# Plain float32 matmuls in a long convolution, a filter stage with angles in turns, and loads made in the stage before

## The chip, the cores and the metric

The kernel runs on one core of one Trainium2 chip. The metric is the device time of one execution in microseconds, the median of several runs. In the profile PE is TensorE, PEld its weight loads, DVE VectorE, ACT ScalarE, POOL GpSimd, SP SyncE, whose queue issues all transfers here.

## The reference

The inputs are x (64 x 64 x 1024, batch, head, position), lengths, the parameters of a state-space filter per head, and three weight matrices. What is computed, cut to its core:

```
dtA = A * dt;  Ct = Cc * (exp(dtA) - 1) / A              # per head h and mode n (64 x 64)
K[h, l] = 2 * sum_n real(Ct * exp(dtA * l))              # one filter of 1024 taps per head
y = causal convolution of x with K along l, + x * D,  masked by length
gate, up = quant(y) @ quant(w_gate).T, quant(y) @ quant(w_up).T      # 1024 -> 2752
h = silu(gate) * up
out = x + quant(h) @ quant(w_down).T                     # 2752 -> 1024
```

quant is fake quantisation to 8 bits: a scale from the largest magnitude of a row, rounding, and the scale again.

## The kernel before

There are three stages, each a block in which every engine has its own program and waits on semaphores; between the blocks all engines meet.

**Filters** (`long_filters`). Parameters lie as 32 x 128 tiles (head pairs by modes), on which VectorE does a chain of some 60 small operations: an exponential by polynomial, the angle reduced modulo a full turn in three parts (`reduce_turns`, lines 52 to 62), then Ct through tanh, sines and two complex products (lines 218 to 251). `tick` makes each of them wait for the one before. TensorE transposes four 32 x 128 tiles to columns (line 342). Then, on 128 x 1024 tiles and in two halves of 16 head pairs, VectorE multiplies angles by positions, reduces them again (line 263), ScalarE takes sines (lines 328, 329; a sine table is loaded after the exponential of line 325), and VectorE and GpSimd build tables. exp(dtA l) is split into a coarse and a fine power, so a filter is a product of two 64-row tables: for each of four banks of PSUM (16 heads), TensorE does 2 x 16 matmuls of 32 x 32 (lines 357 to 361), rows 0 to 63 for even heads, rows 64 to 127 for odd ones. ScalarE copies each bank out (line 335) and SP stores it to k_rev in device memory (line 162).

**Convolution and weights** (`convolve_and_pack`), 32 tiles of two heads. For each head (a half tile, `hh`) the filter is loaded as a Toeplitz matrix t of 128 x 1024 whose row p starts one element later (line 510), and x, loaded as 64 rows, is transposed to 128 x 512 (line 861). The convolution (line 875) is, for 8 distances of blocks, a matmul of a 128 x 128 block of t with 512, 448, ... 64 columns of u. To keep accuracy each operand is split in a high part that fits TensorE's reduced float32 type (float32r) and a rest: t_hi (ScalarE, line 657), t_lo (GpSimd, line 611), u_hi (ScalarE, line 663), u_lo (VectorE, line 780), and three matmuls are done per distance. There is one pair of t slots and one x buffer, so the load of the next t waits for t_lo and that of the next x for the transposes. VectorE masks the result (line 788), takes the largest magnitude (line 804), TensorE transposes that (line 899), VectorE makes scales (lines 793 to 800), TensorE spreads the inverse (line 903), VectorE multiplies and rounds to xq (lines 810, 814), SP stores it.

Beside this the weights are quantised and transposed: in tiles 0 to 21 one tile of w_gate and one of w_up each, in tiles 23 to 30 one of w_down (maxima on VectorE, lines 743 to 755; rounding on ScalarE, line 669; back to integers on GpSimd, line 626; transposes on TensorE, line 894; copies on ScalarE, line 683). The order on each engine is written out by hand in its `body(i, par)`. TensorE's is: convolve half 0, transpose of y_max of the tile before, transposes of the next x, transposes of weights, convolve half 1, spread of the inverse, transposes of x, transposes of weights.

**Feed-forward** (`feed_forward`), 32 tiles of 128 rows: bf16 matmuls against weights that lie in on-chip memory whole.

## Time and profile before

| | us |
|---|---|
| median of 3 runs | 1432.2 |
| lowest, highest | 1426.31, 1437.16 |
| profiled execution | 1423.75 |
| its span | 1422.0 |
| TensorE busy in the span | 1298.7 (91%) |
| VectorE busy | 1000.0 (70%) |
| ScalarE busy | 466.8 (33%) |
| GpSimd busy | 490.2 (34%) |

The busy shares are means over three stages with different limits. The page's chain of work that ended last is nearly all in the feed-forward stage, since TensorE works there without a gap, and says little on the first 500 us. Matmuls are pipelined: a record's length has a drain in it that overlaps the next record, so the distance of two starts tells the cost of one in a train, not its length.

### The profile page before, as it was taken

The numbers are of one execution on the slowest core, as the hardware profiler recorded it, in microseconds if no ns is written. First come the engines' busy times: TensorE is split into PE (matmuls) and PEld (weight loads), VectorE is DVE, ScalarE is ACT, GpSimd is POOL, SyncE is SP. The second block draws the span as 40 slices with busy tenths as digits, with TensorE's granted clock in tenths as the row PEclk, the third lists the DMA queues.
The fourth block names the chain that finished last, engine by engine and source line by source line (L and its number), as shares of the span: only waits on it lengthen the run. The fifth ranks groups of instructions, "written<-read, shape, count | busy, mean of one in ns | idle before, by whom it ended". The sixth has DMA issues, their size and how long they took to land.

```text
span 1422.0 us, 21733 instructions
## 1 busy us (share of the span) xinstructions
PE 1298.7 (91%) x7444; PEld 769.8 (54%) x7444; DVE 1000.0 (70%) x1617; ACT 466.8 (33%) x665; POOL 490.2 (34%) x343
## 2 busy tenths in 40 slices
PE   2378888888888799999999999999999999999998
PEld 0377777878878644444444444444444444444443
DVE  7658889798899766556765676567656765676565
ACT  1145555555565322222222222222222222222222
POOL 2257666676677411222122212221222121212220
PEclk9999999999999899999999999999999999999999
DMA  0087776777787422323322332233223322332222
GB/s 4 8 249 232 217 233 199 235 213 215 252 267 236 164 59 65 63 65 70 90 62 65 70 87 65 65 70 87 65 65 70 85 66 65 70 83 68 65 64 74
DMA packets 137599, 161.58 MB, mean 114 GB/s; under 512 B 101644, under 2 KB 101854, under 8 KB 136286
## 3 DMA queue, kind: packets, MB, share of 16 engines
q1 hardware_dynamic: 137566, 161.16, 40.9%
q8 instruction: 18, 0.29, 0.1%
q14 instruction: 15, 0.12, 0.0%
HBM read 113.28 MB, written 25.49 MB: 98 GB/s over the span
## 4 chain that ended last, share of the span: by engine, by line
PE 64%; DVE 0%; ACT 0%; issue 0%
PE ps_o L1113 22%; PE ps_g L1088 21%; PE ps_u L1088 21%; PE ps_t L1098 0%; ACT h_t L1216 0%; DVE ps_o L1168 0%; DVE res L1171 0%
## 5 line engine op out<-in xcount | busy, mean ns | idle before, releaser
L1242 POOL TENSOR_TENSOR h_int<-h,rounder 128x512 bf16<-128x512 f32 x186 | 186.7, 1025 | 698.2 <-ACT h L1207 695.5
L1088 PE MATMUL ps_g<-wgu,rows 128*128 128x512 bf16 (+1 forms) x1536 | 330.8, 359 | 4.5 <-PEq L377 4.5
L1088 PE MATMUL ps_u<-wgu,rows 128*128 128x512 bf16 (+1 forms) x1536 | 329.0, 357 | 0.0
L1113 PE MATMUL ps_o<-wd,h_t 128*128 128x512 bf16 (+1 forms) x1408 | 319.1, 380 | 0.0
L1201 ACT ACTIVATE g_buf<-g_buf 128x512 f32<-128x512 f32 x192 | 112.3, 585 | 596.3 <-DVE g_buf L1139 596.3
L1139 DVE SCALAR_TENSOR_TENSOR g_buf<-ps_g,sx_all,wide 128x512 f32<-128x512 f32 x192 | 132.3, 689 | 242.4 <-PE ps_g L1088 242.4
L1088 PEld LDWEIGHTS ps_g<-wgu,rows 128*128 128x128 bf16 x1536 | 145.0, 98 | 163.6 <-issue 13.2
L1113 PEld LDWEIGHTS ps_o<-wd,h_t 128*128 128x128 bf16 (+1 forms) x1408 | 134.2, 98 | 178.0 <-issue 34.4
L1088 PEld LDWEIGHTS ps_u<-wgu,rows 128*128 128x128 bf16 x1536 | 146.9, 98 | 151.6 <-issue 0.8
L611 POOL TENSOR_TENSOR t_lo<-t_raw,t_hi 128x1024 fp32r<-128x1024 f32 x64 | 162.5, 2540 | 81.2 <-ACT t_hi L657 81.2
L875 PE MATMUL ps_y<-u_hi,t_hi 128*128 128x512 f32 (+7 forms) x512 | 171.8, 336 | 8.1 <-POOL t_lo L611 3.5
L1139 DVE SCALAR_TENSOR_TENSOR u_buf<-ps_u,sx_all,wide 128x512 f32<-128x512 f32 x192 | 132.4, 690 | 63.1 <-PE ps_u L1088 63.1
L875 PE MATMUL ps_y<-u_lo,t_hi 128*128 128x512 f32 (+7 forms) x512 | 170.2, 332 | 0.0
L875 PE MATMUL ps_y<-u_hi,t_lo 128*128 128x512 f32 (+7 forms) x512 | 168.6, 329 | 0.0
L1207 ACT ACTIVATE h<-h,h_inv 128x512 f32<-128x512 f32 x192 | 118.4, 664 | 80.5 <-DVE h_inv L1160 80.5
L626 POOL TENSOR_TENSOR w_int<-wide,rounder 128x1024 bf16<-128x1024 f32 (+1 forms) x68 | 124.5, 1836 | 54.1 <-ACT wide L669 45.1
L1149 DVE TENSOR_TENSOR h<-g_buf,u_buf 128x512 f32<-128x512 f32 x192 | 138.8, 723 | 0.0
L1151 DVE TENSOR_REDUCE h_max<-h 128x1 f32<-128x512 f32 x192 | 121.1, 631 | 6.6
L875 PEld LDWEIGHTS ps_y<-u_hi,t_hi 128*128 128x128 f32 x512 | 104.6, 204 | 15.0 <-issue 8.2
L875 PEld LDWEIGHTS ps_y<-u_lo,t_hi 128*128 128x128 f32 x512 | 104.1, 203 | 4.9
L875 PEld LDWEIGHTS ps_y<-u_hi,t_lo 128*128 128x128 f32 x512 | 103.5, 202 | 4.9
L657 ACT ACTIVATE t_hi<-t_raw 128x1024 fp32r<-128x1024 f32 x64 | 67.6, 1056 | 116.7 <-DMA t_raw<-k_rev 116.3
(149 smaller groups left out, 1024.5 us busy)
## 6 DMA issues: line engine op xcount, KB each, us to landing
t_raw<-k_rev SPq DMA_DIRECT2D x64, 512.0 KB, 5.9
rows<-in_x SPq DMA_DIRECT2D x64, 256.0 KB, 3.9
res<-in_x SPq DMA_DIRECT2D x64, 256.0 KB, 3.9
out_x<-res SPq DMA_DIRECT2D x64, 256.0 KB, 3.2
wide<-in_L_ffn_w_gate SPq DMA_DIRECT2D x22, 512.0 KB, 6.2
wide<-in_L_ffn_w_up SPq DMA_DIRECT2D x22, 512.0 KB, 7.4
wide<-in_L_ffn_w_down SPq DMA_DIRECT2D x8, 1376.0 KB, 7.6
xq_dram<-xq SPq DMA_DIRECT2D x32, 256.0 KB, 5.8
```

What stands on the lines that cost most here:

```text
L611: pool.tensor_tensor(t_lo[:, hh, :], t_raw[:, hh, :], t_hi[:, hh, :].bitcast(F32), ALU.subtract).then_inc(t_lo_done, 1)
L626: pool.tensor_tensor(out, src, rounder[:].to_broadcast([P, out.shape[1]]), ALU.subtract).then_inc(w_int_ready, 1)
L657: act.activation(t_hi[:, hh, :], t_raw[:, hh, :], ACT.Copy).then_inc(t_hi_done, 1)
L875: last = pe.matmul(out[:, dist * B:NC * B], t[:, hh, block_cols], u[:, hh, 0:n], start=(dist == 0 and k == 0), stop=(dist == NC - 1 and k ...
L1088: last = pe.matmul(bank[:, 0:n], xq[:, par, c, :], wgu[:, NC - 1 - c, first + cols.start:first + cols.stop], start=(c == 0), stop=(c == NC ...
L1113: last = pe.matmul(ps_o[o][:], h_t[0:width, c, :], wd[0:width, c, o * W:(o + 1) * W], start=(c == 0), stop=(c == FC - 1))
L1139: dve.scalar_tensor_tensor(out=buf[:, j % 2, 0:n], in0=bank[:, 0:n], scalar=sx, in1=s[:, cols], op0=ALU.mult, op1=ALU.mult).then_inc(gu_sc ...
L1149: dve.tensor_tensor(h[:, par, cols], g_buf[:, j % 2, 0:n], u_buf[:, j % 2, 0:n], ALU.mult).then_inc(h_ready, 1)
L1151: dve.tensor_reduce(h_max[:, par, j:j + 1], h[:, par, cols], X, ALU.max, apply_absolute_value=True).then_inc(h_maxed, 1)
L1201: act.activation(g_buf[:, j % 2, 0:n], g_buf[:, j % 2, 0:n], ACT.Silu).then_inc(silu_done, 1)
L1207: act.activation(h[:, par, cols], h[:, par, cols], ACT.Copy, scale=h_inv[:, par:par + 1], bias=ROUND).then_inc(h_rounded, 1)
L1242: pool.tensor_tensor(h_int[:, piece(j)], h[:, par, piece(j)], rounder[:].to_broadcast([P, n]), ALU.subtract).then_inc(h_int_ready, 1)
```

## The change

In the filter stage: the angle is kept as a fraction of a turn, so that the large tiles are reduced with one rounding and one subtraction in place of six operations, and the factor 2 pi is the scale of ScalarE's sine; a part of the small products goes to GpSimd, started before ScalarE's results are there; the last matmuls alternate between the two halves of the rows instead of finishing one bank after the other; working tiles move to the memory of wgu, so that the buffers of the next stage are free. SP loads x and weights of tiles 0 and 1 in this stage, and, once the first two banks are stored, their t.

In the convolution stage: one plain float32 matmul per distance on t as loaded and u as copied, in place of three; t has four slots and x two buffers. t_hi, t_lo, u_lo and their semaphores go.

```diff
-def reduce_turns(dve, tick, phase, turns, bound):
+def reduce_turns(dve, tick, phase, angle, turns, bound):
 ...
+def load_toeplitz(sp, k_rev, toep, t_loaded, i, par, hh, L, KROW):
+    slot = 2 * par + hh
+    src = bass.AP(tensor=k_rev.tensor, offset=(2 * i + hh) * KROW, ap=[[1, P], [1, L]])
+    sp.dma_start(toep[:, slot, :], src).then_inc(t_loaded[slot], 16)
+def load_rows(sp, x, x_bufs, x_loaded, i, par, B):
+    for hh in range(2):
+        sp.dma_start(x_bufs[par][hh * B:(hh + 1) * B, :],
+                     x[:, bass.ds(2 * i + hh, 1), :].squeeze(1)).then_inc(x_loaded[par], 16)
 ...  long_filters, SP
+            for i in range(2):
+                load_rows(sp, x, x_bufs, x_loaded, i, i, B)
+            for i in range(2):
+                for g, w in enumerate((w_gate, w_up)):
+                    sp.dma_start(w_f32[:, unit_slot(d, i, g)], w[i * P:(i + 1) * P, :]).then_inc(w_loaded[2 * i + g], 16)
             sp.wait_ge(consts_ready, 1)
 ...
             for b in range(len(ps_k)):
+                if b == 2:
+                    sp.wait_ge(k_stored, 48)
+                    for i in range(2):
+                        for hh in range(2):
+                            load_toeplitz(sp, k_rev, toep, t_loaded, i, i, hh, L, d["KROW"])
 ...  VectorE, small tiles
-            tick(dve.tensor_scalar(s(HALF), s(BB), 0.5, None, ALU.mult))
-            reduce_turns(dve, tick, s(HALF), s(TURN), 3.1415925)
+            reduce_turns(dve, tick, s(RED), s(BB), s(TURN), 3.1415925)
+            tick(dve.tensor_scalar(s(FRAC), s(RED), 1.0 / (2 * math.pi), None, ALU.mult))
 ...
+            dve.wait_ge(pool_small, 3)
+            tick(dve.reciprocal(s(NORM), s(NORM)))
+            for part in (W_RE, W_IM):
+                tick(dve.scalar_tensor_tensor(out=s(part), in0=s(part), scalar=2.0, in1=s(NORM), op0=ALU.mult, op1=ALU.mult))
             dve.wait_ge(act_small, 3)
 ...
-            (lines 231 to 251: norm, its reciprocal, two complex products, scalings)
+            tick(dve.scalar_tensor_tensor(out=s(T0), in0=s(IM), scalar=-1.0, in1=s(W_IM), op0=ALU.mult, op1=ALU.mult))
+            tick(dve.tensor_tensor(s(CT_RE), s(RE), s(W_RE), ALU.mult))
+            tick(dve.tensor_tensor(s(CT_RE), s(CT_RE), s(T0), ALU.add))
+            tick(dve.tensor_tensor(s(T0), s(RE), s(W_IM), ALU.mult))
+            tick(dve.tensor_tensor(s(CT_IM), s(IM), s(W_RE), ALU.mult))
+            tick(dve.tensor_tensor(s(CT_IM), s(CT_IM), s(T0), ALU.add))
 ...  large tiles
-            for kind in range(2):
-                tick(dve.tensor_tensor(phase[:, kind], over(1), powers[:, kind], ALU.mult))
             for half, hs in enumerate(halves):
-                reduce_turns(dve, tick, phase[:, :, hs], turns[:, :, hs], 3.1415925)
+                for kind in range(2):
+                    tick(dve.tensor_tensor(phase[:, kind, hs], over(1)[:, hs], powers[:, kind, hs], ALU.mult))
+                tick(dve.tensor_scalar(turns[:, :, hs], phase[:, :, hs], ROUND, ROUND, ALU.add, ALU.subtract))
+                tick(dve.tensor_tensor(phase[:, :, hs], phase[:, :, hs], turns[:, :, hs], ALU.subtract))
 ...  GpSimd
+            for out, left, right in ((NORM, s(A_RE), s(A_RE)), (N_IM, a_im[:], a_im[:]),
+                                     (W_RE, c_re, s(A_RE)), (C0, c_im, a_im[:]),
+                                     (W_IM, c_im, s(A_RE)), (C1, c_re, a_im[:])):
+                pool.tensor_tensor(s(out), left, right, ALU.mult).then_inc(pool_products, 1)
+            pool.wait_ge(pool_products, 6)
+            (three sums and differences of these)
 ...  TensorE
+            for half in range(2):
+                for j in range(HB):
+                    for hp in range(2):
+                        rows = slice(N * hp, N * hp + N)
+                        pe.matmul(ps_k[2 * half + hp][:, j, :], high_re[rows, first + j, :], cosine[rows, 1, first + j, :],
+                                  start=False, stop=False, skip_group_check=True)
+                    for hp in range(2):
+                        ...  the same with high_im and sine, stop=True
 ...  convolve_and_pack, SP
-                    sp.wait_ge(x_turned, 2 * i + 4)
-                    load_x(i + 2)
-                    sp.wait_ge(t_lo_done, 2 * i + 3)
-                    load_t(i + 2, 0)
+                    sp.wait_ge(x_turned, 2 * i + 2)
+                    load_x(i + 2, par)
+                    sp.wait_ge(conv_done, 2 * i + 1)
+                    load_t(i + 2, par, 0)
 ...
-                    sp.wait_ge(t_lo_done, 2 * i + 4)
-                    load_t(i + 2, 1)
+                    sp.wait_ge(conv_done, 2 * i + 2)
+                    load_t(i + 2, par, 1)
 ...  TensorE
-                    parts = ((t_hi, u_hi), (t_hi, u_lo), (t_lo, u_hi))
-                    for k, (t, u) in enumerate(parts):
-                        last = pe.matmul(out[:, dist * B:NC * B], t[:, hh, block_cols], u[:, hh, 0:n],
-                                         start=(dist == 0 and k == 0), stop=(dist == NC - 1 and k == 2),
-                                         skip_group_check=True)
+                    last = pe.matmul(out[:, dist * B:NC * B], toep[:, slot, block_cols], u[:, hh, 0:n],
+                                     start=(dist == 0), stop=(dist == NC - 1), skip_group_check=True)
```

## Rows read from the trace of the kernel before

**Rows 1.** Busy times by stretch: engines, clock, DMA share, GB/s.
```profile
70.46:97.54 27.08, 17.85 (x120) 16.53 (x120) 12.64 (x19) 12.09 (x14) 14.91 (x7) 1.00 0.80 241
97.54:368.47 270.93, 235.12 (x1744) 214.34 (x1744) 230.68 (x353) 144.91 (x167) 184.89 (x84) 0.92 0.72 223
368.47:484.37 115.90, 103.03 (x781) 92.79 (x782) 103.58 (x140) 67.79 (x78) 85.12 (x42) 0.94 0.71 227
...
499.07:1422.00 922.93, 916.10 (x4502) 426.46 (x4502) 592.16 (x998) 229.07 (x392) 186.79 (x187) 1.00 0.30 70
```

**Rows 2.** TensorE's waits, 97.54 to 368.47 us: total, times, longest.
```profile
PE ps_m L899 <- DVE y_max L804: 22.3, 13, 2.3
PE ps_m L899 <- DMA rows<-in_x: 8.9, 7, 2.1
```

**Rows 3.** Timeline of TensorE, one half tile: start, length, what.
```profile
122.15 0.30 PE L899 MATMUL ps_m<-ident,y_max 128*128 128x128 f32 x1 [0.64 <-DVE u_lo L780]
...
123.45 0.47 PE L875 MATMUL ps_y<-u_hi,t_hi 128*128 128x512 f32 x1
...
126.99 0.28 PE L875 MATMUL ps_y<-u_hi,t_lo 128*128 128x64 f32 x1
127.10 0.36 PE L903 MATMUL ps_i<-diag,ones 128*128 128x128 f32 x1
```

**Rows 4.** VectorE's groups, 97.54 to 368.47 us: busy, mean ns, idle before.
```profile
L804 DVE TENSOR_REDUCE y_max<-y 128x128 f32<-128x1024 f32 x21 | 41.3, 1965 | 0.0
L814 DVE TENSOR_SCALAR xq<-y 128x1024 bf16<-128x1024 f32 x21 | 31.4, 1496 | 2.3
L788 DVE TENSOR_TENSOR y<-ps_y,mask 128x512 f32<-128x512 f32 x42 | 28.9, 687 | 5.1 <-PE ps_y L875 4.1
L780 DVE TENSOR_TENSOR u_lo<-ps_x,u_hi 128x512 fp32r<-128x512 f32 x42 | 28.7, 684 | 27.9 <-ACT u_hi L663 27.9
L810 DVE TENSOR_TENSOR y<-y,ps_i 128x1024 f32<-128x1024 f32 x21 | 25.4, 1211 | 0.0
```

**Rows 5.** Timeline of TensorE, the plain float32 matmuls of line 347.
```profile
25.49 7.03 PE L347 MATMUL ps_k<-d_rows,last_one 1*32 1x512 f32 x8
```

**Rows 6.** Timeline of TensorE, the plain float32 matmul of line 903.
```profile
258.80 0.47 PE L903 MATMUL ps_i<-diag,ones 128*128 128x128 f32 x2
259.20 0.71 PE L861 MATMUL ps_x<-ident,rows 64*128 64x64 f32 x8
```

**Rows 7.** Timeline of the filter stage's small operations.
```profile
14.13 0.21 DVE L218 TENSOR_SCALAR small<-small 32x128 f32<-32x128 f32 x1 [0.63 <-ACT small L322]
...
18.05 0.28 DVE L231 TENSOR_TENSOR small<-small 32x128 f32<-32x128 f32 x1
...
18.99 0.94 DVE L234 RECIPROCAL small<-small 32x128 f32<-32x128 f32 x1
...
24.96 0.60 PE L342 MATMUL ps_cols<-ident,small 32*128 32x32 f32 x4 [24.96 <-DVE small L251]
```

**Rows 8.** Timeline of the filter stage's large tiles.
```profile
33.79 1.28 ACT L328 ACT_TABLE_LOAD   x1
...
38.61 1.04 ACT L329 ACTIVATE cosine<-wide 128x1024 f32<-128x1024 f32 x1
...
43.61 1.23 DVE L270 SCALAR_TENSOR_TENSOR cosine<-cosine 128x1024 f32<-128x1024 f32 x1
```

**Rows 9.** Timeline of the end of the filter stage and the next start.
```profile
59.03 1.64 DVE L281 TENSOR_TENSOR wide<-wide 128x512 f32<-128x512 f32 x1
...
67.66 0.59 ACT L335 ACTIVATE wide<-ps_k 32x512 f32<-32x512 f32 x1 [2.64 <-PE ps_k L360]
...
70.46 0.35 SPq L510 DMA_DIRECT2D t_raw<-k_rev  x1
...
77.70 1.60 PE L861 MATMUL ps_x<-ident,rows 64*128 64x64 f32 x16 [10.14 <-DMA rows<-in_x]
80.32 0.77 PE L875 MATMUL ps_y<-u_hi,t_hi 128*128 128x512 f32 x1 [1.02 <-DVE u_lo L780]
```

More of the change, by code:

```diff
@@ L49, in split_dims, with unit_slot @@
     )
[L52 removed]
+def unit_slot(d, par, u):
+    start = par * (2 * d["F"] - 2 * d["L"]) + u * d["L"]
+    return slice(start, start + d["L"])
+def reduce_turns(dve, tick, phase, angle, turns, bound):
     c1 = 6.28125
@@ L57, in reduce_turns @@
     c3 = 2 * math.pi - c1 - c2
-    tick(dve.tensor_scalar(turns, phase, 1.0 / (2 * math.pi), ROUND, ALU.mult, ALU.add))
+    tick(dve.tensor_scalar(turns, angle, 1.0 / (2 * math.pi), ROUND, ALU.mult, ALU.add))
     tick(dve.tensor_scalar(turns, turns, ROUND, None, ALU.subtract))
-    for part in (c1, c2, c3):
-        tick(dve.scalar_tensor_tensor(out=phase, in0=turns, scalar=-part, in1=phase, op0=ALU.mult, op1=ALU.add))
+    for source, part in ((angle, c1), (phase, c2), (phase, c3)):
+        tick(dve.scalar_tensor_tensor(out=phase, in0=turns, scalar=-part, in1=source, op0=ALU.mult, op1=ALU.add))
     tick(dve.tensor_scalar(phase, phase, bound, -bound, ALU.min, ALU.max))
+def load_toeplitz(sp, k_rev, toep, t_loaded, i, par, hh, L, KROW):
[6 more added lines that the diff above has]
+                     x[:, bass.ds(2 * i + hh, 1), :].squeeze(1)).then_inc(x_loaded[par], 16)
 def long_filters(nc, d, log_dt, C, log_A_real, A_imag, D, lengths, k_rev, ident, ones, identb, rounder, mask, scratch,
-                 rows):
+                 x, w_gate, w_up, w_f32, toep, x_bufs, t_loaded, x_loaded, w_loaded):
     H, B, L, NC = d["H"], d["B"], d["L"], d["C"]
@@ L95, in long_filters @@
         size = 2 * H2 * R
-        phase, turns = (scratch[:, k * size:(k + 1) * size].rearrange("p (k h r) -> p k h r", k=2, h=H2)
-                        for k in range(2))
-        decay = sb("decay", [P, 2, H2, R])
-        sine = sb("sine", [P, 2, H2, R])
-        cosine = sb("cosine", [P, 2, H2, R])
-        high_re = scratch[:, 2 * size:2 * size + H2 * R].rearrange("p (h r) -> p h r", h=H2)
-        high_im = rows[:].rearrange("p (h r) -> p h r", h=H2)
+        phase, turns, decay, sine, cosine, high = (
+            scratch[:, k * size:(k + 1) * size].rearrange("p (k h r) -> p k h r", k=2, h=H2) for k in range(6))
+        high_re, high_im = high[:, 0], high[:, 1]
         d_row = sb("d_row", [1, H])
@@ L140, in over, with s @@
             return cols[:, k, :].unsqueeze(2).to_broadcast([P, H2, R])
+        (A_RE, A, FRAC, RED, TURN, TANH, EM1, EXPA, RE, IM, SIN, COS, NORM, T0, CT_RE, CT_IM,
+         W_RE, W_IM, N_IM, C0, C1, BB) = range(22)
+        def s(k):
+            return small[:, k, :]
         count = [0]
@@ L317, in _ @@
         def _(act):
-            act.wait_ge(dve_step, reached["half"])
-            act.activation(small[:, 10, :], small[:, 3, :], ACT.Sin).then_inc(act_small, 1)
-            act.activation(small[:, 11, :], small[:, 3, :], ACT.Sin, scale=0.5).then_inc(act_small, 1)
-            act.activation(small[:, 5, :], small[:, 1, :], ACT.Tanh, scale=0.5).then_inc(act_small, 1)
+            act.wait_ge(dve_step, reached["reduced"])
+            act.activation(s(SIN), s(RED), ACT.Sin, scale=0.5).then_inc(act_small, 1)
+            act.activation(s(COS), s(RED), ACT.Sin, scale=0.25).then_inc(act_small, 1)
+            act.activation(s(TANH), s(A), ACT.Tanh, scale=0.5).then_inc(act_small, 1)
             flat = "p k h r -> p (k h r)"
@@ L340, in _ @@
             pe.wait_ge(dve_step, reached["small"])
-            for k, src in enumerate((1, 2, 14, 15)):
-                last = pe.transpose(ps_cols[:, k, :], small[:, src, :], ident[0:H2, 0:H2])
+            for k, src in enumerate((A, FRAC, CT_RE, CT_IM)):
+                last = pe.transpose(ps_cols[:, k, :], s(src), ident[0:H2, 0:H2])
             last.then_inc(cols_done, 1)
@@ L392, in convolve_and_pack @@
         s_rows = sb("s_rows", [GU_UNITS + DOWN_TILES, P])
-        t_raw = sb("t_raw", [P, 2, L])
-        t_hi = sb("t_hi", [P, 2, L], F32R)
-        t_lo = sb("t_lo", [P, 2, L], F32R)
-        u_hi = sb("u_hi", [P, 2, NC * B], F32R)
-        u_lo = sb("u_lo", [P, 2, NC * B], F32R)
+        u = sb("u", [P, 2, NC * B])
         y = sb("y", [P, 2, NC, 2, B])
@@ L652, in _, with take_u @@
         def _(act):
-            def t_high(i, hh):
-                act.wait_ge(t_loaded[hh], 16 * i + 16)
-                if not isinstance(i, int) or i >= 1:
-                    act.wait_ge(conv_done, 2 * i + hh - 1)
-                act.activation(t_hi[:, hh, :], t_raw[:, hh, :], ACT.Copy).then_inc(t_hi_done, 1)
-            def u_high(i, hh):
+            def take_u(i, hh):
                 act.wait_ge(x_turned, 2 * i + hh + 1)
@@ L814, in quantise_y @@
                 dve.tensor_scalar(xq[:], v, ROUND, ROUND, ALU.add, ALU.subtract).then_inc(xq_ready, 1)
-            for hh in range(2):
-                u_low(0, hh)
             first_max(0, 0)
```

163 lines of the change are left out of this document (58 added, 105 removed).

## The prediction, made before the change was run

> **What bounds the kernel now.** I read the busy times by stage first [rows 1]. The stretch from 499.07 us on, 923 us, is the feed-forward stage: TensorE is busy for 916 us of it at full clock, and nothing in the change touches it. All that can move lies in the 499 us before: the filter stage up to 70.46, the start of the convolution stage up to 97.54, and then that stage proper, whose cuts at 97.54, 368.47 and 484.37 are the starts of the 1st, 22nd and 31st transpose of y_max (line 899, one per tile). So 21 tiles that also prepare gate and up weights take 270.93 us, 12.90 us each, and the next nine take 115.90, 12.88 each.
>
> Then I asked what a period is made of. TensorE is idle for 270.93 - 235.12 = 35.8 us [rows 1], 1.70 per tile, nearly all of it before the y_max transpose, for y_max itself or for the x rows [rows 2]. The granted clock is 0.92, so 8% of 12.90, 1.03 us per tile, is lost to the lower level (1.2 GHz). Work at full clock is the rest, 12.90 - 1.70 - 1.03 = 10.17 us. A half tile at full clock confirms it: y_max transpose at 122.15, first convolution matmul at 123.45, next step at 127.10, so 1.3 us of transposes and 3.65 us of convolution [rows 3]. In the nine later tiles the same sum is 12.88 - 1.43 (idle) - 0.77 (clock 0.94) = 10.68 us.
>
> VectorE is the other long engine. In those 21 tiles it waits 27.9 us for u_hi and 4.1 for convolutions [rows 4], 1.5 per tile, so its serial work is 11.4 us. TensorE and VectorE wait for each other in turns; neither is saturated.
>
> **The convolution arithmetic.** Removed per half tile: ScalarE's copy to t_hi, GpSimd's subtraction t_lo, VectorE's u_lo (0.68 us [rows 4]), and 24 reduced float32 matmuls. Added: 8 plain float32 matmuls. A plain one appears as two records: the 4 matmuls of 512 columns at line 347 are 8 records in 7.03 us [rows 5], 0.85 us each with the last one's drain. That is 1024 columns at 1.2 GHz (an estimate; the clock column reads 1.00 there, but TensorE had done nothing until then and the spacing tells more), two passes per record. At full clock a record of n columns should take 2n / 2.4 GHz, 0.43 us for 512. A weight load of 128 columns sets a floor: the records at 126.99 and 127.10 start 0.11 us apart, with only 64 columns between them [rows 3]. With 15 ns of overhead per record, a half tile is 2 x (0.115 + 0.122 + 0.175 + 0.228 + 0.282 + 0.335 + 0.388 + 0.442) = 4.17 us for n = 64 to 512, against 3.65: **+0.52 us per half**. The lower bound is the pure stream of 2304 columns in four passes, 3.84 us. The upper bound is the plain pair at line 903: 0.40 us from its start to the next instruction, where 128 columns need 0.21 [rows 6]; if all 8 matmuls kept that 0.19 us, a half would take 5.35. I take 4.17: the pair stands alone before a change of row group, while a train of matmuls can load under the stream, as the reduced one does.
>
> **Waits and buffers.** x gets a second buffer, so its load is released a tile earlier, ahead of the waits for convolutions on SP's queue, and the x part of [rows 2] goes. t gets four slots that are matmul operands as loaded; a slot's load waits for conv_done and has nearly two tiles, over 20 us, until its use. Behind that wait on SP stand the second weight load and the xq store, both wanted a tile later. DMA was 0.72 busy at 223 GB/s [rows 1]; the same bytes in 11.2 us make 0.83, about what the start already shows (0.80). What of y_max? After a second half's convolution VectorE does mask 0.69, quantise 1.2 and 1.5, reduction 2.0 [rows 4], 5.4 us. TensorE has 0.4 + 1.1 + 4.17 = 5.7 us of its own before it asks for y_max, so that wait should all but vanish. VectorE's work falls to 11.4 - 2 x 0.73 = 9.9 us, and with t_lo gone GpSimd is less in its way. Without waits I expect the full clock, as in the long dense stage.
>
> Period with gate and up weights: 10.17 + 1.04 = 11.2, gain 21 x 1.7 = **35.7 us**. The nine others: 9 x (10.68 + 1.04) = 105.5, plus 3.6 us for the waits for scale rows, which I leave in: 109.1 against 115.9, gain **6.8 us**. The last half: +0.5.
>
> **The filter stage.** VectorE's small operations are serial, 0.31 us each. Those from 18.05 to 24.96 (6.9 us [rows 7]) make way for six (1.9) and, earlier, for a reciprocal (0.97) and two more (0.63), of which 0.63 us falls into the idle time before 14.13. Nine operations go to GpSimd, which idles there. The added scaling replaces a removed one. Gain 6.9 - 1.9 - 1.6 + 0.6 = 4.0. From 24.96 on VectorE needed 18.65 us, until 43.61, for both halves' phases [rows 8]. The new first phase is two multiplies of 512 columns, a rounding and a subtraction: 3.3 us by the widths of [rows 4], twice that if GpSimd is in the way. So ScalarE binds: its table load ends 10.1 us after 24.96, two sines of 1.05 add 2.1, and VectorE goes on 12.2 us after instead of 18.65: gain 6.4. The 17.1 us of tables stay. They end at 60.67 - 10.4 = 50.3.
>
> Alternating row halves: the last two banks' 64 matmuls (128 records) took about 6.9 us in order, 54 ns per record, before the last copy at 67.66 [rows 9]. Alternated, both banks end together, and two copies of 0.59 follow: +0.6 if nothing overlaps, -2.8 if two row halves run side by side. No row shows the alternation; the nearest are these, so I take +0.6.
> By the Trainium skill, "TensorEngine Tiling (Array Packing)", rules on tiles, different tiles can load weights and multiply in parallel; by it the stage would end 3.4 us sooner than in my sum, and no row here shows it.
>
> **The start.** The next block begins at 50.3 + 9.8 + 0.6 = 60.7 in place of 70.46, if the early loads don't delay the last k_rev stores. SP issues eight loads of x and weights at its beginning, 0.35 us or a little more each [rows 9], long before the first bank is copied; the four t loads, 2.1 MB, come between the stores, 8.7 us at 241 GB/s [rows 1], about the time until the last stores: nothing, or up to 3 us. With x, t and weights in place the convolution waits only for transposes of x and one copy: 80.32 - 77.70 less u_lo, 1.9 us, instead of 9.86. The first half runs at the low level as now: 7.7 us by [rows 5]. Then 1.3, 4.2, 1.3, 4.2, and y_max 0.4, together 21.0. The first y_max transpose comes at 81.7 instead of 97.54: gain **15.8 us**.
>
> Sum: -35.7 - 6.8 - 15.8 + 0.5 = **-58 us**. The profiled execution took 1423.75 (span 1422.0), 8.5 below the median of 1432.2. It would become 1366, the median 1374.
>
> **Rivals.**
> VectorE stays the pace (0.20): if GpSimd holds the xq operation up so that y_max comes 6.6 us after the convolution, TensorE waits 0.9 in each tile, the period is 12.1, the gain 30 x 0.8 + 16 = 40: 1392. For it: y_max is the largest wait today. Against it: 1.3 us of slack per tile, and more than half of GpSimd's work gone.
> The plain matmul's fixed cost is not hidden (0.07): halves of 5.35, period 13.6, 30 x 0.7 - 16 + 3 = +8: 1440, no difference. For it: [rows 6]. Against: [rows 9], where short plain records follow each other without a gap.
> The clock (0.06), the case of a slower kernel: if each tile's first half, which follows 1.3 us of light transposes, ran at 1.2 GHz it would take 7.7 us and the period 14.7: 30 x 1.8 - 16 = +38, 1470. It decides from a mean half of 5.4 us, a third of each at the low level. Against it: what precedes the low level today is a wait, and the waits go.
> The early loads push the k_rev stores out, or half of the filter gain fails (0.07): 1374 + 8 = 1382.
>
> **Numbers.** Forecast 1374 at 0.60, its own range 1356 (halves of 3.84 us, row halves side by side) to 1388 (halves of 4.4). The 8-in-10 range is 1353 to 1404: it takes in VectorE's case and the late stores, and leaves out the two cases of a long convolution. A measurement of this kernel can tell about 1%, 14 us, from nothing: faster by more 0.87, within 0.07, slower 0.06.
>
> **What would show it.** Right: convolution halves of 4.2 us, a granted clock above 0.97 and TensorE idle for under 0.3 us per tile in the stage proper, first convolution matmul near 62.6 us, periods of 11.2 and 11.7. Wrong: halves over 5 us, a clock of 0.9, or waits of a microsecond for y_max.

## The result: 1352.0 us, and the profile after

The changed kernel takes 1352.04 us (median of 4 runs, 1351.77 to 1353.31) where the kernel before took 1432.92 in the same comparison (1426.31 to 1437.16): ratio 0.9441, 95% interval 0.9404 to 0.9478. The gain is 81 us. I had forecast 1374 and a range from 1353, so the result lies 1 us below the range. The direction and the main mechanisms were right; the sizes were not, nearly all to the same side.

The profiled execution took 1353.31 with a span of 1351.2, against 1423.75 and 1422.0 before. Busy times by stretch come first; the cuts are again the starts of the y_max transposes of tiles 1, 22 and 31 (columns as in [rows 1]).

```profile
57.90:78.82 20.92, 18.75 (x97) 12.84 (x97) 9.96 (x14) 8.47 (x10) 7.53 (x4) 0.78 0.50 157
78.82:305.06 226.24, 226.24 (x1409) 162.87 (x1409) 176.60 (x310) 107.17 (x124) 75.72 (x40) 1.00 0.92 267
305.06:412.97 107.91, 102.85 (x639) 73.08 (x639) 88.27 (x122) 51.94 (x60) 44.17 (x24) 1.00 0.78 227
```

The 21 tiles with gate and up weights take 226.24 us, 10.77 each where [rows 1] gave 12.90. TensorE is busy for all of it at clock 1.00: the waits of [rows 2] and the lost clock are both gone. The nine later tiles take 11.99 each in place of 12.88. The first y_max transpose starts at 78.82 in place of 97.54. The feed-forward stage is as before. Three stretches make up nearly the whole change of the span, in us:

| | forecast | measured |
|---|---|---|
| 21 tiles | -35.7 | -44.7 |
| nine tiles | -6.8 | -8.0 |
| until the first y_max transpose | -15.8 | -18.7 |
| last half, end | +0.5 | +0.6 |
| span | -58 | -70.8 |

One tile on TensorE, from y_max transpose to y_max transpose (start, length, what), answers to [rows 3]:

```profile
78.82 0.28 PE L873 MATMUL ps_m<-ident,y_max 128*128 128x128 f32 x1
...
80.13 4.16 PE L850 MATMUL ps_y<-u,toep 128*128 128x512 f32 x16
84.13 0.44 PE L877 MATMUL ps_i<-diag,ones 128*128 128x128 f32 x2
...
85.60 4.16 PE L850 MATMUL ps_y<-u,toep 128*128 128x512 f32 x16
89.59 0.28 PE L873 MATMUL ps_m<-ident,y_max 128*128 128x128 f32 x1
```

The convolution half goes from 80.13 to 84.13, 4.00 us from start to start (4.16 includes the last one's drain). Its weight loads show why it isn't 4.17:

```profile
204.59 0.19 PEld L850 LDWEIGHTS ps_y<-u,toep 128*128 128x128 f32 x1 [0.24 <-issue]
205.02 0.19 PEld L850 LDWEIGHTS ps_y<-u,toep 128*128 128x128 f32 x1 [0.24 <-issue]
205.39 0.19 PEld L850 LDWEIGHTS ps_y<-u,toep 128*128 128x128 f32 x1 [0.19 <-issue]
```

Between the loads for 512 and for 448 columns lie 0.43 us, then 0.37: 2 x 512 and 2 x 448 columns at 2.4 GHz take 0.427 and 0.373. Nothing is left for an overhead per record; what the half takes above the pure stream of 3.84 us comes from the records of 64 columns, which follow each other at 0.11 to 0.12 us as the weight loads do in [rows 3]. VectorE's groups in the same 226 us answer to [rows 4]:

```profile
L788 DVE TENSOR_REDUCE y_max<-y 128x128 f32<-128x1024 f32 x21 | 40.6, 1933 | 0.0
L772 DVE TENSOR_TENSOR y<-ps_y,mask 128x512 f32<-128x512 f32 x42 | 28.9, 687 | 43.4 <-PE ps_y L850 43.4
...
L798 DVE TENSOR_SCALAR xq<-y 128x1024 bf16<-128x1024 f32 x21 | 14.6, 694 | 2.3
L784 DVE TENSOR_SCALAR diag<-ident,t_inv 128x128 f32<-128x128 f32 x21 | 6.0, 286 | 0.7
```

u_lo is gone, and the same xq operation takes 694 ns in place of 1496. VectorE now waits 43.4 us for convolutions, 2.07 per tile, so its serial work is 10.77 - 2.07 = 8.7 us a tile; TensorE alone sets the pace. Last, the filter stage and the start (timeline of VectorE, TensorE and ScalarE):

```profile
23.05 0.29 DVE L276 COPY cols<-ps_cols 128x128 f32<-128x128 f32 x1 [0.86 <-PE ps_cols L373]
...
33.54 1.23 DVE L290 SCALAR_TENSOR_TENSOR wgu<-wgu 128x1024 f32<-128x1024 f32 x1
...
50.65 0.32 PE L391 MATMUL ps_k<-wgu 64*32 64x32 f32 x4 [4.92 <-DVE wgu L301]
...
54.14 1.06 ACT L366 ACTIVATE wgu<-ps_k 32x512 f32<-32x512 f32 x2 [7.26 <-PE ps_k L395]
...
59.78 1.57 PE L837 MATMUL ps_x<-ident,rows 64*128 64x64 f32 x16 [5.73 <-PEq L94]
61.64 6.96 PE L850 MATMUL ps_y<-u,toep 128*128 128x512 f32 x16 [0.29 <-ACT u L655]
68.53 0.71 PE L837 MATMUL ps_x<-ident,x_more 64*128 64x64 f32 x8
```

The last 64 matmuls run from 50.65 to the copy at 54.14, 3.5 us, where the order before took 6.9 [rows 9]. The block starts at 59.78, the first convolution at 61.64.

### The profile page after: what moved, and what is told of

Same layout as the page of the kernel before. It is cut to its first block, busy times and chain, and to the rows that moved or that the text cites. A ratio compares the mean times of both kernels' runs of the same rounds, so it can differ in the third digit from the quotient of the medians.

```text
span 1351.2 us, 20322 instructions
## 1 busy us (share of the span) xinstructions
PE 1284.5 (95%) x6932; PEld 687.5 (51%) x6932; DVE 918.9 (68%) x1536; ACT 409.4 (30%) x601; POOL 335.5 (25%) x288
## 4 chain that ended last, share of the span: by engine, by line
PE 68%; DVE 0%; ACT 0%; issue 0%
PE ps_o L1087 23%; PE ps_g L1062 22%; PE ps_u L1062 22%; PE ps_t L1072 0%; ACT h_t L1190 0%; DVE ps_o L1142 0%; DVE res L1145 0%
## 5 line engine op out<-in xcount | busy, mean ns | idle before, releaser
L850 PE MATMUL ps_y<-u,toep 128*128 128x512 f32 (+7 forms) x1024 | 269.4, 417 | 2.3 <-ACT s_rows L719 1.0
L1062 PEld LDWEIGHTS ps_g<-wgu,rows 128*128 128x128 bf16 x1536 | 145.0, 98 | 163.6 <-issue 13.2
L850 PEld LDWEIGHTS ps_y<-u,toep 128*128 128x128 f32 x1024 | 177.5, 192 | 89.5 <-issue 58.1
L630 POOL TENSOR_TENSOR w_int<-wide,rounder 128x1024 bf16<-128x1024 f32 (+1 forms) x68 | 127.4, 1884 | 222.2 <-ACT wide L661 160.2
L772 DVE TENSOR_TENSOR y<-ps_y,mask 128x512 f32<-128x512 f32 x64 | 44.1, 689 | 70.8 <-PE ps_y L850 68.4
L655 ACT ACTIVATE u<-ps_x 128x512 f32<-128x512 f32 x64 | 38.1, 597 | 136.3 <-PE ps_x L837 136.3
L661 ACT ACTIVATE wide<-wide,w_inv 128x1024 f32<-128x1024 f32 x44 | 50.2, 1144 | 39.9 <-DVE w_inv L758 39.9
L788 DVE TENSOR_REDUCE y_max<-y 128x128 f32<-128x1024 f32 x32 | 61.6, 1926 | 0.1
L1142 DVE SCALAR_TENSOR_TENSOR ps_o<-ps_o,h_s,s_down 128x512 f32<-128x512 f32 x64 | 48.0, 750 | 9.9 <-DMA res<-in_x 8.3
L1145 DVE TENSOR_TENSOR res<-ps_o,res 128x512 f32<-128x512 f32 x64 | 44.2, 691 | 2.2
```

Of the source, the lines that this page charges most:

```text
L630: pool.tensor_tensor(out, src, rounder[:].to_broadcast([P, out.shape[1]]), ALU.subtract).then_inc(w_int_ready, 1)
L661: act.activation(w_f32[:, cols], w_f32[:, cols], ACT.Copy, scale=w_inv[:, par, u:u + 1], bias=ROUND).then_inc(w_rounded, 1)
L788: dve.tensor_reduce(y_max[:], y[:, par].rearrange("p c h b -> p (h b) c"), X, ALU.max, apply_absolute_value=True).then_inc(y_max_done, 1)
L850: last = pe.matmul(out[:, dist * B:NC * B], toep[:, slot, block_cols], u[:, hh, 0:n], start=(dist == 0), stop=(dist == NC - 1), skip_group ...
L1062: last = pe.matmul(bank[:, 0:n], xq[:, par, c, :], wgu[:, NC - 1 - c, first + cols.start:first + cols.stop], start=(c == 0), stop=(c == NC ...
```

## The experiments

Medians are in us. The kernel before, measured again beside each group of runs, had 1431.9 to 1432.3 with the first twelve kernels and 1435.9 with the last three (e13 to e15); the ratio is against it. Theory A is each time the account that I held, drawn from the prediction and the trace after.

**1. The parts alone.** First the new filter stage without early loads, on the old convolution:

```diff
 (before) + long_filters and reduce_turns of the change, no early loads of x, weights, t
```

> The kernel before with the new filter stage alone (angles in turns, products on GpSimd, alternating row halves), without the loads in it, and the old convolution stage. Theory A (the filter stage's gain passes through whole and has nothing to do with the convolution): the convolution stage's first load is issued at 57 us instead of 70.46, the period per tile stays at 12.9 us, the time is 13 us lower, 1420. Rival (the start of the convolution stage swallows it): 1432. If the 81 us of the whole change came mostly from here, it would be 1352.

Measured 1422.4 (1412.8 to 1431.9), ratio 0.9891 (0.983 to 0.9952). The first y_max transpose came at 85.63, 11.9 sooner, but the 21 tiles then took 13.65 each in place of 12.90 at a clock of 0.88 in the profiled execution, which was the slowest of the four. The old loop, in which two engines wait for each other and the clock falls, is unsteady (the four executions lie 19 us apart), and in the profiled one it gave back more than the start had gained; the median kept 9.5 us.

Then the buffers alone, with all arithmetic as before: four t slots, but still one x buffer, each half of which is reloaded as soon as it has been transposed.

```diff
-        t_raw = sb("t_raw", [P, 2, L]);  t_lo = sb("t_lo", [P, 2, L], F32R)
+        t_raw = sb("t_raw", [P, 4, L], F32R)          # t_lo is written over it
-                    sp.wait_ge(t_lo_done, 2 * i + 3)
+                    sp.wait_ge(conv_done, 2 * i + 1)   # and x reloaded half by half
```

> The kernel before with its three reduced float32 matmuls and all the splitting kept, but with four t slots (t_lo written over the raw slot) and each half of x reloaded as soon as that half has been transposed; filter stage as before. Theory A (the wait for each other of TensorE and VectorE was a matter of late loads as well as of VectorE's work): the x waits go, and VectorE's own serial work of 11.4 us per tile becomes the period: 11.5 instead of 12.9, 42 us less, 1390. Rival B (buffers are all): period 10.2, TensorE's own work, 1350. Rival C (the splitting work on VectorE and GpSimd is all): period 12.5, 1420.

Measured 1407.1, ratio 0.982 (0.9766 to 0.9874): between A and C. Its windows, VectorE's groups and TensorE's waits over 21 tiles:

```profile
100.00:361.72 261.72, 232.16 (x1745) 212.65 (x1745) 247.20 (x351) 145.89 (x167) 183.21 (x83) 0.92 0.77 232
```
```profile
L815 DVE TENSOR_SCALAR xq<-y 128x1024 bf16<-128x1024 f32 x21 | 36.5, 1740 | 2.3
L801 DVE TENSOR_SCALAR diag<-ident,t_inv 128x128 f32<-128x128 f32 x21 | 30.6, 1457 | 0.7
```
```profile
PE ps_m L900 <- DVE y_max L805: 28.5, 19, 2.3
```

The waits for x rows are gone, and VectorE takes their place: it waits for convolutions for 6.2 us in all, so its work is (261.72 - 6.2) / 21 = 12.2 us a tile, where it was 11.4 in the kernel before. The two operations above account for it: they took 1496 [rows 4] and 770 ns before,

```profile
L800 DVE TENSOR_SCALAR diag<-ident,t_inv 128x128 f32<-128x128 f32 x21 | 16.2, 770 | 0.7
```

1740 and 1457 here, and 694 and 286 after the change. Buffers alone were worth 25 us; the rest needs the arithmetic. Between the profiled executions it is 17.8 us, and 11.2 of them lie in the nine later tiles, which took 11.64 us each in this run, less than the 11.99 after the whole change.

**2. The matmul itself.** Three reduced matmuls per distance as before, but on unsplit operands, so that only TensorE's part of the old arithmetic is there (values less accurate):

```diff
+                    for k in range(3):
+                        last = pe.matmul(... start=(dist == 0 and k == 0), stop=(dist == NC - 1 and k == 2))
```

> The changed kernel with three reduced float32 matmuls per distance on the unsplit operands in place of the one plain float32 matmul (the values are less accurate; nobody splits). It has the matmuls of before and the waits, buffers and helpers of after. Theory A (in the changed kernel TensorE alone sets the period of 10.77 us, and a plain half costs 4.00 us against 3.65): period 10.07, 31 x 0.7 = 22 us less, 1330. Rival (DMA, 0.92 busy at 267 GB/s between the cuts, is the bound just behind): period stays above 10.5, 1345 or more.

Measured 1331.2, ratio 0.9277 (0.9232 to 0.9322), period 10.05, with the DMA engines 0.96 busy at 286 GB/s: the rival in which they bound the loop just behind TensorE is out. The plain matmul is thus the dearer one by 0.73 us a tile, 0.36 per half: 4.00 against the 3.65 of [rows 3]. The gain of the change comes from what surrounds the matmuls, in spite of them.

**3. The other engines' work put back**: VectorE's operation of 512 columns per half, GpSimd's of 1024, or both.

```diff
+    dve.tensor_tensor(u_extra[:, hh], ps_x[hh][:], mask[:], ALU.mult)               # VectorE's
+    pool.tensor_tensor(t_extra[:], t_extra[:], t_extra[:], ALU.subtract)            # GpSimd's
```

> The changed kernel with one more VectorE operation of 512 columns per half tile at the place of u_lo (0.69 us, it reads the transposed x in PSUM, and TensorE waits for it before the next transposes, as before). Theory A: VectorE waits 2.07 us per tile in the changed kernel, 1.45 more work fits in it in the 21 gate tiles, the period stays 10.77; in the nine others, where it already makes TensorE wait 0.6 us, up to 1.4 each: 1352 + 0 to 12, 1358. Rival C (VectorE's work passes through whole): 31 x 1.4 = 43 us more, 1395.

> The changed kernel with only GpSimd's extra operation per half tile. Theory A (what GpSimd's work costs is VectorE's time, 2.2 us per tile at most): VectorE 8.7 + 2.2 = 10.9 us per gate tile against TensorE's 10.77: period 10.8 to 11.1, 1352 + 2 to 10, 1358. Rival (GpSimd's work doesn't touch VectorE): 1352.

> The changed kernel with both helpers' work put back as idle work: VectorE's operation of 512 columns per half tile at u_lo's place, and a GpSimd operation of two 1024-column float32 operands per half tile at t_lo's place; convolution, buffers and early loads as changed. Theory A (VectorE becomes the bound as in the kernel with buffers only, where the xq and diag operations took 1.74 and 1.46 us beside GpSimd instead of 0.69 and 0.29): 8.7 + 1.45 + 2.2 = 12.4 us per gate tile, 34 us more in all, 1390. Rival (the work fits into VectorE's 2.07 us of waiting, as alone): 1360.

Measured: VectorE's 1358.6 (0.9467), GpSimd's 1371.2 (0.9571), both 1365.5 (0.9535). I had expected 1358 of GpSimd's, and both to cost most. VectorE's met its number (1358) but not its reason: I had put all of the cost in the nine later tiles, and it lies in the 21, whose period is 11.04 (5 us), with 1 us in the nine. In the 21 tiles of the run with GpSimd's operation alone:

```profile
L813 DVE TENSOR_SCALAR xq<-y 128x1024 bf16<-128x1024 f32 x21 | 46.2, 2198 | 2.3
```
```profile
PE ps_m L888 <- DVE y_max L803: 15.3, 20, 0.9
...
DVE y L787 <- PE ps_y L865: 30.7, 22, 3.8
```

and with both:

```profile
L820 DVE TENSOR_SCALAR xq<-y 128x1024 bf16<-128x1024 f32 x21 | 33.0, 1570 | 2.3
```
```profile
PE ps_m L903 <- DVE y_max L810: 9.8, 19, 0.6
...
DVE y L794 <- PE ps_y L880: 2.5, 3, 1.4
```

VectorE has 30.7 us to spare with GpSimd's alone, and yet TensorE waits for it in 20 of 21 tiles. It isn't VectorE's sum of work that costs there but one chain: the quantising operation, held up by GpSimd, stands right ahead of the maximum that TensorE's next transpose needs. With both put back it is the sum: VectorE waits only 2.5 us, its work is 11.29 us a tile, and the period is 11.41. That xq is held up less there (1570 ns), so that both cost less than GpSimd's alone, I put down to VectorE coming to it at another moment; no run isolates that. If the chain is what costs with GpSimd's alone, it must go when the maximum is taken first:

```diff
-                if last_one:
-                    max_y(i, par)
+                max_y(i, par)
                 ...  quantise_y(i - 1, 1 - par)
-                if not last_one:
-                    max_y(i, par)
```

> The kernel with GpSimd's subtraction put back (1371.2: 19 us more than the kernel after the change, 15.3 of them as TensorE's waits for y_max), and VectorE taking the maximum before it quantises. Theory A: GpSimd's work costs time only through the quantising operation, which it slows from 0.7 to 2.2 us and which stands ahead of the maximum that TensorE waits for; with the maximum first that chain is cut: at most 1358, period at most 11.0 in the 21 tiles, waits for y_max gone. Theory B: GpSimd's work slows something else that TensorE needs (the mask multiplies, its own scaled transposes, ScalarE): the time stays at 1366 to 1371, period 11.5 or more.

Measured 1355.9, ratio 0.9461 (0.9432 to 0.949), period 10.89:

```profile
L813 DVE TENSOR_SCALAR xq<-y 128x1024 bf16<-128x1024 f32 x21 | 26.6, 1267 | 2.3
L799 DVE TENSOR_SCALAR diag<-ident,t_inv 128x128 f32<-128x128 f32 x21 | 24.5, 1165 | 0.8
```
```profile
PE ps_m L885 <- DMA x_more<-in_x: 0.9, 2, 0.5
```

The hold-ups are still there (xq and diag 2.4 us a tile, against 0.98 without GpSimd's operation), but no wait for y_max is left. That is theory A: of GpSimd's 19 us, 15 went through this chain.

**4. One x buffer**, as before, all else as after:

```diff
-            x_bufs = (rows, x_more)
+            x_bufs = (rows, rows)
-                    sp.wait_ge(x_turned, 2 * i + 2)
+                    sp.wait_ge(x_turned, 2 * i + 4)
```

> The changed kernel with one x buffer, each load released by the transposes of the tile before, as in the kernel before. Theory A (a wait costs twice: itself, and the lower clock after it): the load has 4.6 us until TensorE wants it and lands after 6.5, so TensorE waits about 2 us per tile, the granted clock falls to about 0.85 and takes another 1 to 1.5 us per tile: period 13.8 to 14.3, 1352 + 31 x 3.2 = 1450. Rival B (waits cost themselves alone): period 12.8, clock 0.98 or more, 1414. Rival C (the second x buffer does nothing): 1352.

Measured 1386.5, ratio 0.9689 (0.9667 to 0.9711), none of the three numbers. Waits of TensorE and VectorE over the 21 tiles:

```profile
PE ps_m L875 <- DVE y_max L790: 13.6, 11, 2.0
PE ps_m L875 <- DMA rows<-in_x: 5.4, 8, 1.4
```
```profile
DVE w_max L741 <- DMA wide<-in_L_ffn_w_up: 38.3, 18, 3.6
```
```profile
78.18:331.79 253.61, 234.99 (x1407) 166.91 (x1408) 192.13 (x310) 105.32 (x124) 75.71 (x40) 0.98 0.75 237
```

The wait for the buffer is in SP's queue, and what suffers is the weight load queued behind it: VectorE waits 1.8 us a tile for w_up, and passes the delay to y_max. The x rows themselves cost TensorE only 5.4 us. The second cost of theory A hardly shows: the clock is 0.98. Of the eleven waits of 1.05 to 2.00 us in these tiles, eight are followed by a convolution half of 4.00 us, as at full clock, and three by one of 4.7 to 5.6. The second x buffer is worth 34 us in this order of SP's queue; in the run with the buffers alone one x buffer, reloaded half by half, left no wait for x in the 21 tiles, so another order might give part of it back. No run tries that on the changed kernel.

**5. The filter stage and the start**, each part undone:

```diff
 (no early loads) the eight loads of x and weights and the four of t issued at the start of the next block
 (bank by bank)   for hp in range(2): for j in range(HB): ...   in place of   for j ...: for hp ...
```

> The kernel after the change, with the eight early loads of x and weights and the four of t taken out of the filter stage and issued at the start of the convolution block. Theory A: nothing else covers them; after the block's start the first convolution waits for a t load again, as before (9.86 us after the block's start in place of 1.9), and the last k_rev stores gain nothing by it: 1352.0 + 8 = 1360, first y_max transpose at about 86.8 in place of 78.8, everything behind it shifted by the same 8 and no more. Theory B: part of the 18.7 us gained at the start came from elsewhere and the early loads also delayed the stores; then the block starts sooner without them and the time is 1353 to 1357.

> The kernel after the change, with the last 64 matmuls of each half of the tables in the old order, one row half's bank after the other's. Theory A: alternated row halves run side by side (3.4 us where the old order took 6.8), so the last two banks end 3.4 us later, of which one copy of 0.6 is saved since the first bank is copied meanwhile: 1352.0 + 2.8 = 1355, first y_max transpose at about 81.6. Theory B: the 3.4 us came from something else (the new scaling of the tables, less waiting): then no change, 1352.

Measured 1359.9 (0.9489) and 1356.4 (0.9466), first y_max transposes at 86.17 and 81.26, periods unchanged at 10.77. ScalarE's copies of the four banks in the run bank by bank:

```profile
45.83 0.59 ACT L366 ACTIVATE wgu<-ps_k 32x512 f32<-32x512 f32 x1 [10.39 <-PE ps_k L393]
49.05 0.59 ACT L366 ACTIVATE wgu<-ps_k 32x512 f32<-32x512 f32 x1 [2.63 <-PE ps_k L393]
54.38 0.59 ACT L366 ACTIVATE wgu<-ps_k 32x512 f32<-32x512 f32 x1 [4.74 <-PE ps_k L393]
57.61 0.59 ACT L366 ACTIVATE wgu<-ps_k 32x512 f32<-32x512 f32 x1 [2.64 <-PE ps_k L393]
```

The second bank of each half follows the first by 3.2 us; alternated, both are there where here only the first is. Row halves do run side by side. (The start has scatter of its own: in nine profiles of kernels with the same filter stage and early loads, the one after the change among them, the first y_max transpose comes between 77.64 and 78.84.) Without early loads the stores of k_rev land in half the time and the block begins sooner (issues of the last two stores: KB each, us to landing; then TensorE's timeline):

```profile
k_rev<-wgu SPq DMA_DIRECT2D x2, 64.0 KB, 1.8
```
```profile
65.52 1.60 PE L837 MATMUL ps_x<-ident,rows 64*128 64x64 f32 x16 [11.22 <-DMA rows<-in_x]
```

After the change they take 3.4 us. The block's first load is issued at 57.68 without early loads, while with them the block begins at 59.78: the early loads push the last stores out by 2.1 us, as the prediction's last rival had it, and save 9.5 of waiting. Loading only tile 0's t early should keep the one without the other:

```diff
-                    for i in range(2):
-                        for hh in range(2):
-                            load_toeplitz(sp, k_rev, toep, t_loaded, i, i, hh, L, d["KROW"])
+                    for hh in range(2):
+                        load_toeplitz(sp, k_rev, toep, t_loaded, 0, 0, hh, L, d["KROW"])
 ...  tile 1's at the start of the next block
```

> The kernel after the change, but only tile 0's two t loads (1 MB) are issued between the k_rev stores; tile 1's follow at the start of the convolution block. Theory A: the early t loads delay the last two stores (3.4 us from issue to landing in place of 1.8 without them); half of them end before the stores begin, so the block begins 2 us sooner, first y_max transpose at 76.8 in place of 78.8, time 1350. Theory B: the stores are slow for another reason, or tile 0's loads alone do the harm: 1352 as before; if tile 1's t then came late for its first convolution, more than that.

Measured 1350.5 (1349.3 to 1351.4), ratio 0.9408 (0.9377 to 0.9438). The stores land in 1.8 us again, and TensorE starts 2.05 sooner:

```profile
57.73 1.57 PE L839 MATMUL ps_x<-ident,rows 64*128 64x64 f32 x16 [3.45 <-PEq L94]
```

The first y_max transpose comes at 75.45, 3.4 sooner, but the median gained only 1.5. The profiled execution of the changed kernel is the slowest of its four and this one the fastest of its six, and the start scatters by 1.2 us, so the 3.4 is the upper side of the gain; what it is exactly stays open.

**6. The nine later tiles.** There TensorE waits 0.5 to 0.6 us for y_max in five tiles after the change. The maximum first:

> The kernel after the change, with VectorE taking the maximum of tile i before it quantises tile i-1, in every tile and not in the last alone. Theory A: TensorE's waits for y_max in the nine later tiles (0.5 to 0.6 each, 5 us of idle time in that stretch in all) come from the quantising operation (up to 2.4 us beside GpSimd) ahead of the maximum; they go, the nine tiles take 11.5 each and the time is 1348; the 21 tiles, in which TensorE never waits, stay at 10.77. Theory B: the maximum comes in time, but TensorE then waits for rows of scales instead, or the quantised tile comes late for its store and the next quantise: 1352 or a little more.

Measured 1352.7, ratio 0.944 (0.9413 to 0.9467): theory B, nothing gained. The waits for y_max are gone, and two tiles take 13.2 us. SP's issues, then TensorE's timeline and the second tile's windows:

```profile
314.16 0.35 SPq L594 DMA_DIRECT2D xq_dram<-xq  x1
...
318.91 0.37 SPq L543 DMA_DIRECT2D wide<-in_L_ffn_w_down  x1
319.58 1.46 SPq L80 DMA_DIRECT2D x_more<-in_x  x2
```
```profile
329.03 0.33 PE L870 MATMUL ps_m<-ident,y_max 128*128 128x128 f32 x1 [1.72 <-DMA x_more<-in_x]
...
330.83 5.86 PE L847 MATMUL ps_y<-u,toep 128*128 128x512 f32 x16
...
338.10 4.21 PE L847 MATMUL ps_y<-u,toep 128*128 128x512 f32 x16
```
```profile
329.03:342.14 13.11, 13.11 (x73) 8.85 (x74) 7.52 (x15) 6.36 (x7) 5.11 (x3) 0.87 0.73 227
```

xq is ready later: its store is issued at 314.16, where after the change it was at 312.73, and what stands behind it on SP's queue is later by nearly the same, w_down's load at 318.91 (317.59) and the x loads at 319.58 (318.26). That x lands at 329.0, behind the 1.4 MB of w_down. TensorE waits 1.72 us for it, and then the granted clock is 0.87 over the tile: one convolution half takes 5.86 in place of 4.16. This wait of 1.7 cost 3.4. So with the x load issued ahead of that store (and thereby ahead of the load of w_down, which this run doesn't separate):

```diff
-                    sp.wait_ge(x_turned, 2 * i + 2)      # at the start of the body
-                    load_x(i + 2, par)                   # (tile 2's stays there)
 ...
+                if has(i, TILES - 3):
+                    sp.wait_ge(x_turned, 2 * i + 4)
+                    load_x(i + 3, 1 - par)
                 ...  store_xq(i - 1)
```

> The kernel with the maximum before the quantising operation (1352.7), and on SP's queue the load of x issued ahead of the store of xq in place of behind it (one tile's body earlier). Theory A: the x load came late only because the store of xq, now ready later, stood ahead of it; the two tiles of 13.2 become 11.4, the nine tiles 11.6 each, time 1348.5 to 1349.5. Theory B: the transfers are late because the DMA engines are full (0.9 busy); then another load comes late and the time stays at 1352 to 1353.

Measured 1350.1 (1348.5 to 1351.2), ratio 0.9403 (0.9373 to 0.9433), the nine tiles 11.60 each, as theory A has it; the time is 0.6 above its upper end.

**7. A faster version.** Transposing two heads' x at once saves eight small matmuls a tile; the first run has the maximum first as well:

```diff
-                for c in range(NC):
-                    last = pe.transpose(ps_x[hh][:, c * B:(c + 1) * B], x_bufs[par][rows, c * P:(c + 1) * P], ident[rows, rows])
+                    last = pe.transpose(ps_x[k][:, j * P:(j + 1) * P], x_bufs[par][:, c * P:(c + 1) * P], ident[:])
```

> A version meant to be faster than the changed kernel: the two heads of a tile are transposed together (8 transposes of 128 x 128 in place of 16 of 64 x 64, u double-buffered), and VectorE takes y_max before it quantises the tile before. Theory A (TensorE alone is the bound in the gate tiles, y_max held up by the xq operation beside GpSimd in the nine others): 0.4 us less per tile, 0.6 us more in the nine: 31 x 0.4 + 9 x 0.6 = 18 less, 1334. Rival (DMA, 0.92 to 0.96 busy): 1345. Rival (one more read order makes TensorE wait for u): 1352 or more.

> Merged transposes of two heads and the maximum first (1350.7), x loads ahead of the store of xq, and only tile 0's t loaded early. Theory A: the two gains add to what was measured: 1350.7 - 2 - 1.5 = 1347. Theory B: neither order matters and it stays at 1350.7.

The first gave 1350.7, ratio 0.9434 (0.9418 to 0.945), far from the 1334 of theory A; its last rival, TensorE waiting for u, came closest. TensorE's work fell by the 0.4 us a tile that I had expected, but the period is 10.71, since TensorE then waits for u 14 times, 5.0 us, and 2.2 us for other things. Joined with the x loads ahead of the store and only tile 0's t early it is 1345.5 (1344.8 to 1345.8), ratio 0.9373 (0.9343 to 0.9403), 6.5 us below the changed kernel's median, which was not measured beside it; period 10.64, nine tiles 11.67.

## Why the prediction was right and wrong

The mechanism held, and three terms of the sum failed. The 8.5 us between profile and median, carried over unchanged, make 9.8 of the 22 us between forecast and result. The 15 ns of overhead per record made a convolution half 4.17 us where it measured 4.00: 7 us in the 21 tiles and 3 in the nine. The start was 2.9 us too long, with the +0.6 for alternated row halves, which measured as a gain of 2.4. And the range was not summed from its own bounds.

**Waits and clock, right.** The prediction said that the x wait would go, that y_max's should all but vanish, and that without waits the clock would be full. TensorE is busy in 226.24 of 226.24 us at 1.00. The run with four t slots and x reloaded half by half shows that earlier loads don't do it without the arithmetic (28.5 us of waits, clock 0.92), and experiment 4 what the second x buffer is worth. In the nine later tiles 2.9 us of waits for y_max stayed.

**"15 ns of overhead per record", wrong.** This was the step that sized the convolution half at 4.17; it measured 4.00. I took the overhead from trains of reduced matmuls, without naming a row for it, and laid it on plain ones, whose weight loads are exactly 2n columns apart. It made 0.34 us a tile too much, 7 of the 9 us in the 21 tiles. The other 2 are the rest of TensorE's work, 2.77 a tile where the subtraction of waits and clock from the period left 10.17 - 7.30 = 2.87. The bounds, 3.84 and 5.35, held. The DMA engines, put at 0.83 busy, were 0.92 and still not the bound.

**VectorE's work, wrong but without effect.** 11.4 less 1.46 made 9.9; it is 8.7, since GpSimd's lighter load also halved two operations that I had left at their duration of before. I said that GpSimd would be less in the way and put no number on it. Experiment 3 gives it one. The rival in which xq is held up and VectorE paces (1392) was real as a mechanism: with GpSimd's work back it appears, at 19 us through the chain and at 13 with both back, where I had priced it at 18.

**Nine tiles, right for two reasons that cancel.** The convolution gained 3.1 us more than forecast there, and 2.9 us of waits for y_max took it back, since xq takes 2.3 to 2.4 us beside GpSimd's long operation on w_down. TensorE's waits in the nine tiles:

```profile
PE ps_m L873 <- DVE y_max L788: 2.9, 5, 0.6
PE ps_y L850 <- ACT s_rows L719: 1.0, 1, 1.0
PE ps_y L850 <- ACT s_rows L723: 0.9, 1, 0.9
```

The 1.2 us left over come from the waits for scale rows, 1.9 in place of the 3.6 that I had left in, less some 0.4 of other work.

**"So I take +0.6", wrong.** For the alternated row halves I had a bound of -2.8 and took the other end. Experiment 5 measures 2.44 us at the first y_max transpose, with the scatter of 1.2 named there (4.3 between the medians, 2.2 between the profiled executions). By the Trainium skill, "TensorEngine Tiling (Array Packing)", key properties, different tiles load weights and multiply in parallel; the trace agrees, 3.5 us in place of 6.9. That error was hidden by another: the early loads were priced at nothing on the last stores, and cost 2.1. Of the 2.9 us by which the start beat the forecast, 1.0 lies before the first convolution, 0.8 in the first half tile (6.9 us in place of 7.7, since the clock rose inside it: its weight loads stand up to 0.85 us apart, twice the 0.43 of full clock, and the last seven pass in 1.2) and 1.1 in the next two.

**The small tiles, right for the wrong reason.** cols is ready 2.6 us sooner (23.34 against 25.96), not 4.0, and VectorE's first table operation starts at 33.54, 10.1 sooner, where 10.4 was forecast.

**The 8.5 us between profile and median, wrong.** I carried it over. The kernel before is unsteady (runs from 1426 to 1442 in these comparisons), and its profiled execution happened to be a fast one; with the new filter stage on the same loop (experiment 1) the profiled one lay 9.5 us above the median instead. The changed kernel has its runs within 1.5 us, and the profiled one is the slowest of them. Offset and its change of sign, 8.5 + 1.3, are nearly half of the 22 us between forecast and result; the other 12.4 are the table's. That the old loop's waits cause the unsteadiness is argued from the spread, not isolated.

**The range.** Its low end took halves of 3.84 us and side-by-side row halves into account by name, but not in sum: 31 x 0.66 = 20 and 3.4 from 1374 make 1350, and the result would have been inside, though the largest error, the 8.5 us, would still not have been in it.

## What to carry to other kernels

When a change takes the waits out of a loop, it can take three things at once, as here: the wait, the clock that fell after it, and the unsteadiness that stands between profile and median; count all three, and the clock from the trace, since the waits of experiment 4 hardly lowered it. An operation that another engine holds up is best placed behind the one that the critical engine waits for, and a load should stand ahead of any store that waits for late results on the same queue. Add the bounds of a range together before stating it.

## What the runs showed of the hardware

- A plain float32 matmul in a train shows as two records, each taking 2n columns at 2.4 GHz (0.43 us for 512, 0.37 for 448), with no overhead per record at these widths; the eight of a half take 4.00 us, and three reduced ones per distance 3.65.
- VectorE's TENSOR_SCALAR on 128 x 1024 float32 takes 694 ns where nothing holds it up; beside more work on GpSimd its mean in 21 tiles rose to as much as 2198 ns, and one on 128 x 128 from 286 to as much as 1457. TENSOR_REDUCE of y (1905 to 1965) and the multiply out of PSUM by the mask (683 to 688) hardly change. By the Trainium skill, "GPSIMD Engine Reference", specifications, GpSimd's memory interface contends with VectorE instructions in a two-port mode or with two inputs in SBUF, the on-chip memory beside PSUM. That the multiplies, which have one input in PSUM, kept their time fits this; whether the two held-up operations ran in a two-port mode no row here shows.
- Waits of up to 0.9 us, 20 times in 21 tiles, left the clock at 1.00. Longer ones had no fixed price: one of 1.72 was followed by a tile at 0.87, and of eleven of 1.05 to 2.00 (experiment 4) three were followed by a slower half and eight were not.
- Two 64-row halves of TensorE, alternated, do 64 matmuls in 3.4 to 3.5 us where one after the other takes 6.8 to 6.9.
- Two stores of 64 KB, issued behind 2.1 MB of loads on the same queue, landed in 3.4 us, and in 1.8 behind none or behind half of them.
